# Where the tensors of a state-space and two-MLP kernel begin in SBUF

## The reference, cut to what matters

```python
xn = layernorm(x)
# first branch: state-space scan (16 states a channel), then a GELU MLP of 512 -> 2048 -> 512
a = xn + ssm_scan(rmsnorm(xn, scale1), A, B, C, D)
a = a + gelu(rmsnorm(a, scale2) @ w1 + b1) @ w2 + b2
# second branch: gated FFN of 512 -> 1408 -> 512; every operand is rounded to FP4 in blocks of 16
q = lambda t: fp4_quant_dequant(t)
f = q(silu(q(xn) @ q(w_gate).T) * (q(xn) @ q(w_up).T)) @ q(w_down).T
out = x + a + f
```

## Time and profile before

| | before |
|---|---|
| median of three runs | 3132.97 us |
| profiled execution, span from the first to the last instruction | 3132.1 us |
| around the span, to the median (3132.97 - 3132.1) | 0.9 us |
| TensorE matmul busy | 3053.1 us, 97% |
| VectorE busy | 2040.8 us, 65% |
| GpSimd busy | 1149.5 us, 37% |
| ScalarE busy | 1086.7 us, 35% |

### The profile page before, as it was taken

The page is one execution under the profiler, slowest core; times in us unless marked ns, Lnnn a source line. Parts: engine busy times, 40 slices in busy tenths (PEclk is TensorE's granted clock), DMA queues, the critical chain, the costliest instruction groups (busy, mean ns, idle before and its releaser), DMA issues.

```text
span 3132.1 us, 43122 instructions
## 1 busy us (share of the span) xinstructions
PE 3053.1 (97%) x14861; PEld 2472.6 (79%) x14861; DVE 2040.8 (65%) x4427; ACT 1086.7 (35%) x1910; POOL 1149.5 (37%) x1097
## 2 busy tenths in 40 slices
PE   5899999999999999999999999999999999999999
PEld 3678888888877777777777788888888888888887
DVE  8798898987777776767777754444445444444442
ACT  5345655644544343343422422212222122221221
POOL 7556656655555545545554210110111111111000
PEclk9999999999999999999999999999999999999999
DMA  4133434356766666666644533333333333333320
GB/s 128 44 88 91 116 114 120 95 137 183 181 180 174 161 155 174 159 161 168 168 95 98 128 72 72 75 73 72 77 68 80 75 68 71 72 74 74 71 61 14
DMA packets 865577, 335.58 MB, mean 107 GB/s; under 512 B 680400, under 2 KB 771792, under 8 KB 862800
## 3 DMA queue, kind: packets, MB, share of 16 engines
q1 hardware_dynamic: 865360, 332.83, 43.4%
HBM read 225.21 MB, written 107.51 MB: 106 GB/s over the span
## 4 chain that ended last, share of the span: by engine, by line
PE 70%; DVE 15%; issue 5%; POOL 5%; ACT 2%; DMA 2%; SPq 1%; DVEq 0%; POOLq 0%; ACTq 0%
PE bank L880 22%; PE bank L896 22%; PE bank L757 14%; PE bank L779 7%; DVE qs L1000 3%; POOL qa L1547 2%; DVE qa L1017 2%; PE bank L820 2%; DVE qs L1011 2%; DVE qa L973 2%; POOL qa L1541 1%; DVE qb L1025 1%; PE bank L727 1%; PE bank L828 1%; DVE sg L965 1%
## 5 line engine op out<-in xcount | busy, mean ns | idle before, releaser
L880 PE MATMUL bank<-hT,Wp 128*128 128x512 f32 x3072 | 739.6, 390 | 2.2 <-DVE Wp L1188 2.2
L896 PE MATMUL bank<-Wp,G 128*128 128x512 f32 x3072 | 737.6, 389 | 0.0
L880 PEld LDWEIGHTS bank<-hT,Wp 128*128 128x128 f32 x3072 | 577.5, 188 | 122.6 <-issue 2.6
L896 PEld LDWEIGHTS bank<-Wp,G 128*128 128x128 f32 x3072 | 576.6, 188 | 119.9
L757 PE MATMUL bank<-XT,Wg 128*128 128x512 f32 (+1 forms) x2148 | 524.6, 393 | 6.8 <-DVE Wd L1032 6.8
L757 PE MATMUL bank<-XT,Wu 128*128 128x512 f32 (+1 forms) x2148 | 515.7, 389 | 15.9 <-DVE sg L965 15.7
L779 PE MATMUL bank<-Wd,HT 128*128 128x512 f32 x2112 | 515.4, 393 | 6.3 <-POOL HT L1555 5.0
L1237 DVE CAST G<-gf 128x512 fp32r<-128x512 f32 x256 | 110.8, 433 | 599.2 <-PE bank L896 580.0
L757 PEld LDWEIGHTS bank<-XT,Wu 128*128 128x128 f32 x2148 | 401.1, 190 | 106.7 <-issue 25.8
L779 PEld LDWEIGHTS bank<-Wd,HT 128*128 128x128 f32 x2112 | 391.9, 188 | 105.6 <-issue 15.4
L757 PEld LDWEIGHTS bank<-XT,Wg 128*128 128x128 f32 x2148 | 398.7, 190 | 95.9 <-DVE Wd L1032 8.8
(11 more groups left out here) (121 smaller groups left out, 2828.3 us busy)
## 6 DMA issues: line engine op xcount, KB each, us to landing
px<-in_L_attn_x_dram SPq DMA_DIRECT2D x128, 256.0 KB, 3.3
xin<-in_L_attn_x_dram SPq DMA_DIRECT2D x128, 256.0 KB, 3.3
sT<-r_K SPq DMA_DIRECT2D x128, 256.0 KB, 4.2
r_Z<-xin SPq DMA_DIRECT2D x64, 256.0 KB, 2.5
r_U<-ub SPq DMA_DIRECT2D x16, 1024.0 KB, 6.6
sU<-r_U SPq DMA_DIRECT2D x32, 512.0 KB, 5.0
r_Y<-sY SPq DMA_DIRECT2D x16, 1024.0 KB, 5.7
xl<-in_L_attn_x_dram SPq DMA_DIRECT2D x64, 256.0 KB, 3.1
```

The source lines that it names most:

```text
L880: ins = e.matmul(bk[:], Wp[f][wh][:, 0, k * P:(k + 1) * P], hT[xh][b % 2][:, k, :], start=(k == 0 and p_ == 0), stop=(k == KD - 1 and p_ = ...
L896: ins = e.matmul(ACC[j][:], G2[gh][:, n % 2, j * P:(j + 1) * P], Wp[f][wh][:, 1, :], start=(f == 0 and p_ == 0), stop=(f == 15 and p_ == 2))
```

## The change

No instruction is added, removed or reordered. Only the places of tensors change:

```diff
         a128 = sbt(ctx, "a128", [P, 2 * NV])
 
+        sbt(ctx, "pad0", [P, (4096 - nc.sbuf_base) // 4])
+
         actx = ExitStack()
@@
         st6 = sbt(actx, "st6", [P, 2, 6])
 
-        sbt(actx, "pad6", [P, 240])
+        sS = sbt(actx, "sS", [P, 4, 32])
+
+        vec = sbt(actx, "vec", [P, 20])
+        rs2 = sbt(actx, "rs2", [P, 2, 4])
+        sbt(actx, "pad6", [P, (196544 - nc.sbuf_base) // 4])
 
         pctx = ExitStack()
@@
         sY = sbt(sctx, "sY", [P, P, 16])
-        sS = sbt(sctx, "sS", [P, 4, 32])
         sB = sbt(sctx, "sB", [P, 2, 4, 32])
@@
         b2r = sbt(mctx, "b2r", [P, D])
-        vec = sbt(mctx, "vec", [P, 20])
-        rs2 = sbt(mctx, "rs2", [P, 2, 4])
```

## The result

The change makes the kernel slower. Five rounds on one chip gave 3144.95 us after (3143.73 to 3147.57) beside 3133.04 us before (3132.84 to 3134.06), a ratio of 1.0039 with a 95% interval of 1.0026 to 1.0051. Forecast were 3132.5 us and "no change"; the time also lies 2 us above the top of the range.

A forecast was written before the change was run, and what follows sets the result against it. TensorE's matmul distance was taken as the bound: 12408 matmuls at 226.6 ns, 2812 us, 90% of the span. The profiled 3132.1 - 0.5 us, plus 0.9 us up to the median, gave 3132.5 us; range 3118 to 3143.

The forecast's parts named there:

- px, sU, hT0 and what follows them lie 64 short of a multiple of 2048, no longer level with the others: Even blocks' line 880: hT0 no longer at Wp's place modulo 2048; taken as 0, upper end 17 us.
- The upper bound: Even blocks' line 880: worst stretched group found, 2.85 us instead of 2.72, for 128 groups 17 us.
- The rival: Line 880 of the 8 even blocks: matmuls stretch, up to 17 us, about 3150; half taken, 3141; chance 11%.
- The moving and stationary operands' move: Matmuls' operands at new starts: moving 0 us (other end 159 us), stationary 0.5 us off (ends 0 and 1.5).
- The 12.8 ns that don't grow with the columns: Every fp32r matmul: a fixed part of 119.7 - 106.9 = 12.8 ns whatever its length, 159 us in all; expected to stay.
- the first rival: MLP and FFN matmuls: the 12.8 ns are the start's price; 79 and 53 us less, about 3000 us; chance 11%.
- the second rival: Head and FFN stops: other engines or DMAs run better at round places, 8 us less, 3125 us; chance 9%.
- The waits of lines 760 and 782: TensorE's waits outside the head: 15.7 us for VectorE, 5.0 us for GpSimd; other engines' new places taken as 0.
- the DMAs: Their rows in SBUF start at other places; queue 43.4% busy, TensorE waits for none; 0 us.
- the tensors in the gap: sS, vec and rs2: same instructions and waits, vec still loaded behind `ssm_done`; no cost counted.
- Nothing is lost per column, so nothing can be won per column: fp32r matmuls: 256 further columns cost 106.9 ns, against 106.7 ns at one column each cycle of 2.4 GHz.
- 110 against 106.7 ns: Float32 turns of 128 columns: their distance was said to agree with the skill's gap of about 2.5 ns.

The follow-up runs named there:

- e2: Small matmul-only kernel varying the stationary operand's start and width, and types: both operands at 1984 226.7 ns, bf16 215.8 ns.
- e5: The changed kernel with hT0 and its group 192 bytes lower, at 1792: 3131.31 us beside 3133.12 us before, ratio 0.9994.
- e10: Small matmul-only kernel, 12 matmuls off by d bytes then 12 level, in turn: a pair takes 5.44 us level, 5.54 us off by 192.
- e9: The changed kernel with the large tensors 64 bytes lower, level with hT0, which stays: 3132.39 us beside 3131.91 us before, ratio 1.0001.
- e1: Small matmul-only kernel varying only the moving operand's start, 512 and 256 columns: 226.7 to 234.3 ns at 512 columns.
- e8: Small matmul-only kernel with 256, 384, 448 and 512 columns, two runs of 256, and 64 stationary columns: level 120.0 ns at 256, 202.6 at 448.
- e7: Small matmul-only kernel, moving operand of 512 columns at every word of 256 bytes past the stationary one's level: 226.6 ns level, 240 ns worst.
- e6: The changed kernel with hT0's group at 196416, 64 bytes past a multiple of 256: 3143.31 us beside 3133.12 us before, ratio 1.0032.

## Why the prediction was wrong

**The step that failed** is "px, sU, hT0 and what follows them lie 64 short of a multiple of 2048, no longer level with the others. ... I take 0". Its evidence was that line 779 streams `Wd` (1376) against `HT` (352) at the common distance, called there "unequal places". They are unequal modulo 2048, but 1376 - 352 = 1024 = 4 x 256, so they are level in the sense that counts (e2, e5). I had no row of an fp32r pair that was off by anything but a multiple of 256; every large operand of the kernel before is level with its partner. So the row bore witness to nothing, and the honest treatment was the one for an unseen case: its bounds, with more weight than 11% on the upper half. What the runs showed in place of 0: each of the 128 pairs of groups in the even blocks, off by 192, takes 5.54 us instead of 5.44 (the changed kernel, e10).

**The upper bound was near the truth, and that was luck.** It was 0.13 us a group of line 880, 17 us, from a level group stretched behind a float32 turn, and no run shows that the two stretches have a common cause. Measured are 0.10 us a pair, 0.08 in line 883 and 0.02 in line 899: 12.8 us, less 1.8 us in the first block, most of them a fall of the clock that the profiled execution before had and the one after hadn't. The rival had the right place and the right sign, and its threshold of 4.1 ns a matmul was passed (6.7 ns in line 883). That some of the loss would fall in line 899 it did not foresee.

**The range** ended at 3143, a little beyond half of that price (3141). Nothing in the rows spoke for half of the 17 us; the whole price would have set the upper end at 3150, and the time lies inside that.

**What held.** The moving and stationary operands' move to multiples of 64 and of 2048 is worth nothing: the odd blocks stay at 2.72 us, and e5 (large operands at multiples of 2048, `hT0` at 1792) and e9 (`Wp`, `G2`, `hT0` and `hT1` at 1984) equal the kernel before. The 12.8 ns that don't grow with the columns stay, so the first rival fell. With a ratio of 0.9994 in e5, whose interval begins at 0.9985, the 8 us of the second rival (0.9975) are excluded too; a gain of up to 4.7 us isn't. The waits of lines 760 and 782, the DMAs and the tensors in the gap moved nothing that the profile shows.

**A premise that was loose.** "Nothing is lost per column, so nothing can be won per column" took the difference between the distances at 512 and 256 columns, 106.9 ns, for the price of 256 columns, and so the fixed part for a constant. The runs give 226.7, 173.3 and 120.0 ns at 512, 384 and 256 columns when level, but 233.3, 174.7 and 113.3 ns off by 192 (e1, e8): there the same subtraction of 256 columns gives 120.0 ns. And level operands of 448 columns take 202.6 ns, 2.6 more than the fixed part of the other three would have it. The fixed part is not one number. The conclusion held only because both of its rows were of level operands.

Nor is the part over the columns simply the time of a weight load that gets shorter with fewer stationary columns: with 64 instead of 128 of them, level, the distance falls from 120.0 to 113.3 ns at 256 moving columns (e8) but rises from 226.7 to 229.9 at 512 (e2). The 32 cycles that the Trainium skill gives ("TensorE: Matmul & The Clock Gate", section "Weight-path perf modes") are stated there for fp8 weights. That they are nearly the 12.8 ns of the level rows shows nothing about fp32r, and the prediction should have said so. Its reading of the section "Back-to-back issue gap" is as loose: "110 against 106.7 ns" takes two cycles for each of the 128 columns of a float32 turn, which that section doesn't state. For bf16 the trace agrees with the section's 2.5 ns: 215.8 ns at 512 columns (e2), which are 213.3 and 2.5.

As the Trainium skill has it ("SBUF — State Buffer", section "Specifications (TRN2)"), SBUF's lines are 16 bytes, and by that rule alone any start at a multiple of 16 would be as good as another. The measurements bear this out for the move of both operands together (e9), but not for 32 and 64 bytes between them, which cost 6.7 and 2.2 ns a matmul in e1.

**What stays open.** Why the period is 256 bytes, why a few odd words such as 28 or 60 bytes are as good as level, why the first matmuls behind a turn between level and off are uneven, and why 256 columns are faster off than level. The runs show these; none shows the mechanism inside.

## What to carry to other kernels

For streams of fp32r matmuls of 512 columns, look at the start of the moving operand minus the start of the stationary one, modulo 256 bytes, and keep it at 0 for every pair that meets (with 256 columns against 128 stationary ones level was the slowest, so measure there); absolute places, multiples of 64 or of 2048, bought nothing. A tensor moved to fill a gap has to be weighed against each operand that it meets on TensorE. And before a row is called a witness for "unequal" or "unaligned", ask for which modulus it is unequal: a row that is level for a smaller one says nothing.

## What the runs showed of the hardware that was not expected

- The distance of fp32r matmuls depends on the difference of the two starts: at 512 columns 226.7 ns level, 228.9 off by 64, 232.3 to 232.6 by 128, 233.3 by 32, 96, 192 or 224, 234.3 by 160, and up to 240 at single words (e1, e2, e7).
- At 256 columns, with 128 stationary ones, the order turns: 120.0 ns level, 113.3 ns off by 192 (e1, e8). In the kernel before, only the last products of the FFN have 256 columns, 119.7 ns and level.
- bf16 with 512 columns (215.8 ns) and plain float32 with 128 (two records 111.7 ns apart) don't depend on the two starts of the moving operand that were tried, 0 and 1984 (e2).
- A narrower stationary operand, level, makes the fp32r distance longer at 512 moving columns, 229.9 ns at 64 and 231.7 at 32 (e2), and shorter at 256, 113.3 ns at 64 (e8).
- A level group of 12 behind one that is off takes 2.73 to 2.77 us instead of 2.72; only its first nine or so distances are uneven (e1, e6, e10).
- After a stop of 2.2 us the granted clock was 0.61 over the next 4.4 us in the kernel before, so that 12 matmuls cost 1.7 us more; after the changed kernel's stop of 1.7 us it stayed at 1.00.
